# A graph layer with linear attention and routed experts: VectorE adds a segment's sums three turns behind its selectors, and normalises ahead of the fourth low half

## What is computed

```python
xn = _layernorm(x)
# graph branch: mean of the edge features by node, then a two-layer network
sums   = segment_sum(edge_attr, src, 6250)
counts = segment_sum(ones, src, 6250)
agg    = sums / maximum(counts, 1.0)
g      = relu(concat([xn, agg, u]) @ W1 + b1) @ W2 + b2
# mixer, 4 layers, each:
h = layernorm(x); x = x + linear_attention(h) @ Wo + bo
h = layernorm(x); x = x + gelu(h @ W1 + b1) @ W2 + b2
# after both branches: layernorm, argmax over 32 experts, that expert's network
```

## Time and profile before

| what | us |
|---|---|
| median of 3 runs | 2988.53 (2984.98 to 2992.48) |
| profiled execution, its own time | 2975.31 |
| its span, first to last instruction | 2973.6 |
| selectors of the last pass, first to last start | 1939.5 to 2497.3 |
| sums of the last pass, first to last start | 1952.6 to 2504.1 |

### The profile page before, as it was taken

How to read it: one execution, slowest core, us unless ns; L and a number is a source line. 1 busy time by engine, 2 the same in 40 slices (tenths; PEclk the granted TensorE clock), 3 DMA queues, 4 the chain that set the end, 5 groups by cost and what they waited for, 6 DMA issues and landing times.

```text
span 2973.6 us, 56289 instructions
## 1 busy us (share of the span) xinstructions
PE 2670.4 (90%) x18946; PEld 2457.3 (83%) x18946; DVE 2115.9 (71%) x4764; ACT 1547.8 (52%) x3001; POOL 1745.3 (59%) x1613
## 2 busy tenths in 40 slices
PE   4988999999989999998999999788888887997098
PEld 2777899999988999997889999788888887997075
DVE  8887667767656666676567767688888886898055
ACT  0555466666545656663566565344444444764066
POOL 2011287777768888886888886154444544221757
PEclk7999999999999999999999999899999998998599
DMA  5001323222232223224223321233323322210343
GB/s 123 28 28 35 89 58 69 62 62 65 56 102 64 64 63 71 57 60 107 66 57 70 63 64 44 60 108 85 85 83 85 85 80 58 62 47 12 84 123 110
DMA packets 255561, 207.89 MB, mean 70 GB/s; under 512 B 165505, under 2 KB 194386, under 8 KB 255277
## 3 DMA queue, kind: packets, MB, share of 16 engines
q1 hardware_dynamic: 197678, 162.55, 20.6%
q0 software_dynamic: 57600, 41.75, 7.2%
HBM read 136.93 MB, written 70.16 MB: 70 GB/s over the span
## 4 chain that ended last, share of the span: by engine, by line
PE 37%; POOL 30%; DVE 14%; issue 13%; ACT 3%; DMA 2%; DVEq 1%; SPq 0%; ACTq 0%; POOLq 0%
PE bank L380 33%; POOL edges_sorted L735 23%; POOL r L713 3%; PE bank L1813 2%; POOL tokens_sorted L800 2%; DVE xh L1275 2%; DVE hidh_lo L1311 1%; DMA staging<-in_edge_attr 1%; DVE staging L1181 1%; POOL ehl L752 1%; DVE oh L1499 1%; PE bank L2266 1%; DVE bn L1266 1%; DVE kmask L1175 1%; DVE res L1283 1%
## 5 line engine op out<-in xcount | busy, mean ns | idle before, releaser
L735 POOL DMA_INDIRECT edges_sorted<-staging,pos_i x850 | 1059.9, 1247 | 253.7 <-issue 238.2
L851 ACT ACTIVATE hid<-bank,b1p 128x250 f32<-128x250 f32 x800 | 331.3, 465 | 390.3 <-PE bank L380 385.1
L380 PE MATMUL bank<-h_hi,w_hi 128*128 128x250 f32 x1600 | 479.2, 300 | 10.5 <-DVE h_lo L1295 10.5
L1311 DVE TENSOR_TENSOR hidh_lo<-hid,hidh_hi 128x500 fp32r<-128x500 f32 x400 | 296.3, 741 | 257.6 <-ACT hidh_hi L857 250.4
L380 PE MATMUL bank<-w_hi,hidh_hi 128*125 128x256 f32 x1600 | 468.6, 293 | 0.4 <-DVE hidh_lo L1311 0.4
L380 PE MATMUL bank<-w_hi,hidh_lo 128*125 128x256 f32 x1600 | 451.5, 282 | 0.0
L380 PE MATMUL bank<-w_lo,hidh_hi 128*125 128x256 f32 x1600 | 450.3, 281 | 0.0
L380 PE MATMUL bank<-h_hi,w_lo 128*128 128x250 f32 x1600 | 447.9, 280 | 0.0
L380 PE MATMUL bank<-h_lo,w_hi 128*128 128x250 f32 x1600 | 444.5, 278 | 0.0
L380 PE MATMUL bank<-wqk,h 128*125 128x256 f32 x1600 | 373.6, 387 | 0.6 <-ACT mbc L902 0.6
L380 PEld LDWEIGHTS bank<-wqk,h 128*125 128x125 f32 x1600 | 300.7, 192 | 45.0 <-ACT h L819 1.0
(11 more groups left out here) (284 smaller groups left out, 5741.1 us busy)
## 6 DMA issues: line engine op xcount, KB each, us to landing
staging<-edges_sorted SPq DMA_DIRECT2D x103, 260.0 KB
staging<-in_edge_attr SPq DMA_DIRECT2D x50, 531.2 KB
queries<-qn SPq DMA_DIRECT2D x100, 250.0 KB
qin<-queries SPq DMA_DIRECT2D x100, 250.0 KB
edges_sorted<-staging,pos_i POOLq DMA_INDIRECT x850
rows_in<-edges_sorted SPq DMA_DIRECT2D x50, 260.0 KB
yin<-tokens_sorted SPq DMA_DIRECT2D x81, 127.0 KB
raw<-in_L_mix_W SPq DMA_DIRECT2D x8, 1024.0 KB, 6.9
```

Of the source, the lines that this page charges most:

```text
L380: return nc.tensor.matmul(o, left, right, start=start, stop=stop, skip_group_check=True)
L735: nc.gpsimd.indirect_dma_start(out=edges_sorted, out_offset=bass.IndirectOffsetOnAxis(ap=pos_i[:, i:i + 1], axis=0), in_=stage[:, slot, j, ...
L851: a = nc.scalar.activation(hid[c % 2][:, j, :], chunks(PH[c % 2])[:, j, :], ACT.Gelu, bias=b1p[:, 2 * c + j:2 * c + j + 1])
L1311: nc.vector.tensor_tensor(hidh[c % 2][1][:, :, :], hid[c % 2][:, :, :], f32(hidh[c % 2][0][:, :, :]), ALU.subtract).then_inc(f_lo, 1)
```

## The change

VectorE adds the sums of segment n - 3 in turn n, not those of n - 4; the tile numbers are read in turns 0 and 3 of a step, not in turns 1 and 4; and one turn after the last segment falls away (there are 156 turns in all, not 157). In the last pass `xh` of group t + 1 is computed ahead of the low half of chunk 3, not behind it. TensorE's, ScalarE's, GpSimd's and SyncE's streams stay as they are.

```diff
             def seg_turn(n):
-                if n >= 4:
-                    if n % 3 == 1:
-                        seg_kinds.update(zip(range(n - 4, n - 1), seg_tiles(n - 4, 3)))
-                    seg_add(n - 4, seg_kinds[n - 4])
+                if n >= 3:
+                    if n % 3 == 0:
+                        seg_kinds.update(zip(range(n - 3, n), seg_tiles(n - 3, 3)))
+                    seg_add(n - 3, seg_kinds[n - 3])
                 if n < ESEGS:
                     seg_prep(n)
...
+                if attention and not later:
+                    attention_normalise(l, t + 1)
                 if forward:
                     hidden_low(l, t, 3)
-                if attention:
+                if attention and later:
                     attention_normalise(l, t + 1)
...
-            for n in range(SEG_STEP * GROUPS + 3, ESEGS + 4):
+            for n in range(SEG_STEP * GROUPS + 3, ESEGS + 3):
                 seg_turn(n)
```

## The result

The changed kernel takes 2962.40 us (median of 4 runs, 2959.37 to 2964.84) where the kernel before takes 2987.34 (4 runs, 2984.98 to 2992.48): ratio 0.9912, 95% interval 0.990 to 0.9925, or 25 us less. The forecast was 17 us less. The two profiled spans differ by 12 us only, 2973.6 and 2961.5, and not because of the last pass. There the last sum starts at 2478.7 in place of 2504.1, 25.4 us earlier. The expert stage behind it, whose code is the same, took 226.5 us (2735 to 2961.5) where it took 213.6 (2760 to 2973.6): one execution's difference, which the medians do not show.

The account below looks back on a forecast made before the run. TensorE was taken as near its limit, with VectorE and it waiting for each other in a loop. -0.64 us a step times 24 (-15.4) and -1.8 made -17.2: 2988.5 to 2971.3 us; 8-in-10 range 2944 to 2989.

Parts of the forecast that it names:

- The sum one turn earlier: VectorE's sums in the last pass: all three TensorE waits for `agg` go, 2.48 us a step, costed at nothing.
- Point 1: VectorE, turn 5 to turn 2: waits of 0.41, 0.51, 0.59 and 1.13 us go, -2.64 us a step.
- Point 2: GpSimd's low halves of turns 0 and 1 now hold up a VectorE without free time: two at 1.0, +2.0 us.
- Point 3: Turn 3, tile-number read behind `ve`: 0 to +0.36 us, taken as 0, ending together with the 0.67 us wait.
- Point 4: Turn 0, tile-number read behind `h_lo` and the bias: taken as 0, up to +1.25 us if `h_lo` still waited.
- Point 5: `xh` ahead of the fourth low half: 0 on VectorE, serves TensorE's transposes; at worst down 3 waits some 0.4 us.
- The tail: Behind the last step, one of the last two TensorE segments leaves the end: -1.8 us, between 0 and -3.
- The floors: Least step times: 20.5 us for VectorE and GpSimd instructions that exclude each other, 19.8 us for TensorE.
- the whole-cover rival: Last pass, TensorE bounds: all 2.48 us a step comes out, -59.5, 2929 us (2945 by the 20.5 floor); chance 0.15.
- the one of a slower kernel by the read: Turns 0 and 3: `h_lo` still waits for `h_hi`, the tile-number read adds time; step +1.38, 3022 us; chance 0.13.
- The order of `xh` that does nothing: Last pass: moving `xh` has no effect, not distinguishable in time if TensorE doesn't wait for `xh`; forecast stands, no chance given.
- rival in which waits only change their name: TensorE waits for `hidh_lo`, `xh` and `h_lo` instead: -0.24 to 0 us a step, about 2985 us; chance 0.20.

## Why the prediction was right, and where it was not

The sign, the place and the mechanism held: TensorE's three waits for `agg` went, VectorE's step became the measure, and 25 us lie inside the range. That the 25 come so near the 17 of the forecast is in part luck: a regular step gained 1.35 us, twice the 0.64 of the sum, and falls of the clock that no part of it foresaw took 7.4 us back. Two of its own signs of being wrong came true as well, a step under 21 us and selectors in turns 0 to 2 at 1.20. By its steps:

- *The sum one turn earlier costs nothing; its waits go.* Right: none of the three waits for `agg` remains in the steps.
- *Point 1, -2.64 us of VectorE's waits.* Wrong in size: -1.14. The waits of 0.41 and 0.59 went, those for `kb` in turns 1 and 2 stayed at 0.46 and 1.04. I had let TensorE, ScalarE and GpSimd run ahead by up to 2 us. TensorE's two new waits show that `xh` and the low half of chunk 3 tie it to VectorE again: its matmuls of turn 0 start 0.91 us earlier against VectorE's sum of turn 0 than before, no more. And I had moved only one end of each wait; VectorE comes earlier too, by 0.72 us in turn 2 where `kb` comes 0.81 earlier.
- *Point 2, two new hits of 1.0, +2.0.* Wrong, and the largest error: none came. Since the waits for `kb` stayed, GpSimd's low halves of turns 0 and 1 kept their nearly free places. Instead a hit moved: the one on turn 5's selector went (-0.79), the one on `hidh_lo` of chunk 3 makes the stretch from turn 4's selector to turn 5's `agg` 4.22 us long where it was 3.46 (+0.76). The waits of -1.14, these two, and 0.08 us of overlap regained at each of the two places where a wait went, make -1.33, the step's -1.35. Points 1 and 2 were both too large, and their errors partly cancel: -0.64 in the sum where -1.33 was measured.
- *Point 3, the read behind `ve`, 0 with up to +0.36.* Right, and shown: 3.25 us with and without it.
- *Point 4, the read at turn 0.* Right: `h_lo` to `agg` is 2238.13 - 2236.94 = 1.19 us, as before.
- *Point 5, the swap, 0 for VectorE, some 0.4 us for down 3.* VectorE's part is right. That it serves TensorE was said, but given no weight: without it the sums alone gain 0.1%, and 0.64% even with the clock kept up, in place of 0.9 and 1.18. The wait of down 3 is 0.93, not 0.4, because the low half takes a hit there.
- *The clock has little to give.* Wrong, and in no rival. Five falls cost 7.4 us: 1.35 x 24 = 32.4 less those, with the tail's 1.7, less 1.2 us by which the first residual stands later, is 25.5; the last sum starts 25.4 us earlier.
- *The tail, -1.8.* 4.8 to 3.1: -1.7.
- *The floors.* The step of 19.1 us with half low halves is under TensorE's supposed floor of 19.8, which left out what a wait costs beyond its idle time, 0.73 us a step; the same holds for the 2.48 us of the whole-cover rival. The floor of 20.5 for the instructions that exclude each other was not reached by any kernel with full low halves, in a mean over its steps.

Of the rivals, the one of a slower kernel by the read fell with its condition: `h_hi` came in time. The order of `xh` that does nothing fell too: 0.9988 without it, 0.991 with it (0.9936 and 0.9882 with the clock kept up in both). Half of the rival in which waits only change their name is true: 1.25 of TensorE's 2.48 us are still there, for `xh` and `hidh_lo`. The rival of the whole cover held for the regular step in half: 1.35 of 2.48.

The rule of the Trainium skill (SBUF — State Buffer, "Who interferes with whom"), that the later of the two instructions fully blocks, agrees with the rows: `hidh_lo` takes 1.66 and 1.67 us where GpSimd's low half had begun, 0.67 where not. It was right as a mechanism; my error was in guessing where the two would meet. Two things the prediction had too narrow. GpSimd is the later one at times and then takes longer itself: its low half of 2218.24 takes 1.42 us beside a selector, so VectorE and GpSimd do not meet only at semaphores. And `xh`, whose only operand of full width is `res`, is hit as well: 1.61 to 1.70 us beside a low half, 0.72 without one, so "two operands in SBUF" doesn't cover all that is hit.

## What to carry to other kernels

When a wait is taken from the bounding engine, look for the wait that the same engine would have next, and move both: here each edit alone was worth 0.1 to 0.2% and the two together 0.9% (0.6, 0.2 and 1.2% once the clock no longer fell). A step of two engines that feed each other can't be summed wait by wait; lay out the whole round with the new order first, and ask which instruction ties the leading engine to the trailing one. And read the granted clock per step after a change of order: a shorter step with its waits close together can lose at the clock what it gains in waiting, and a few idle matmuls in the wait bring it back.

## What the runs showed of the hardware

TensorE's granted clock fell from 2.4 to 1.2 GHz for some 3 us although it was busy 93% of the last pass (505.67 of 545 us). In the kernel before, three waits of 0.41, 0.99 and 1.08 us a step, spread over the step, brought no fall between 2000 and 2480 us; neither did waits of 1.25 and 0.98 us some 11 us apart, in the kernel with the swap alone. Two waits of 0.32 and 0.93 us within 2 us of each other, with less waiting in all, brought one in every four or five steps; one wait of 1.91 us brought one in nearly every second step. Filled with idle matmuls, which left waits of about 0.3 us and none over 0.6, neither brought any. The sum of the waits in a step thus doesn't tell whether the clock falls; whether their nearness does, or what TensorE runs between them (here the four transposes of `xh`), these runs leave open.
